# Two graph convolutions on one core: the order of a software-pipelined step, and a running maximum taken in another form

## The reference, cut to what matters

```
q = x @ qw + qb;  k = x @ kw + kb;  v = x @ vw + vb          # 8 heads of 16 channels
alpha = sum(q[dst] * k[src], channels) * SCALE               # one number an edge and head
m     = segment_max(alpha, dst)
a     = exp(alpha - m[dst]);  a = a / segment_sum(a, dst)[dst]
out   = segment_sum(v[src] * a, dst) + x @ sw + sb
...
h = relu(conv(x));  h = conv(h);  x = layernorm(x + h)
```

## Time and profile before

| | us |
|---|---|
| median of 3 runs | 3101.77 (3098.66 to 3106.87) |
| the profiled execution's own time | 3101.67 |
| its span, first to last instruction | 3099.9 |
| TensorE, busy | 2460.4 (79%) |
| VectorE, busy | 2586.2 (83%) |
| ScalarE, busy | 1926.8 (62%) |
| GpSimd, busy | 1987.3 (64%) |

### The profile page before, as it was taken

One profiled execution on the slowest core, in us unless ns is written; L12 is line 12 of the kernel. 1 busy time (PEld: TensorE's weight loads), 2 busy tenths in 40 slices (PEclk: granted clock), 3 DMA queues, 4 the chain that ended last, 5 costly groups with the idle time before them and its releaser, 6 DMA issues. The chain is left out here.

```text
span 3099.9 us, 46510 instructions
## 1 busy us (share of the span) xinstructions
PE 2460.4 (79%) x14327; PEld 1739.5 (56%) x14327; DVE 2586.2 (83%) x3231; ACT 1926.8 (62%) x3501; POOL 1987.3 (64%) x1891
## 2 busy tenths in 40 slices
PE   7899999959999996888888589999999961445620
PEld 3466666637777764565666356677777751223410
DVE  6689999969999996999999646898999885999940
ACT  0067677646666665988889557777777733455520
POOL 4477777714334326777777377788778416777776
PEclk9999999979999998999999899999999975657765
DMA  7456767656777765777777436799989777985311
GB/s 210 117 172 217 227 214 225 219 177 194 217 215 214 213 197 175 238 235 229 230 230 233 137 120 170 196 241 220 218 206 245 183 190 246 293 283 159 96 52 39
DMA packets 495871, 611.80 MB, mean 197 GB/s; under 512 B 67257, under 2 KB 285827, under 8 KB 495500
## 3 DMA queue, kind: packets, MB, share of 16 engines
q1 hardware_dynamic: 433814, 495.64, 53.2%
q0 software_dynamic: 56480, 111.88, 13.9%
q10 hardware_dynamic: 5334, 1.32, 0.2%
HBM read 391.94 MB, written 220.55 MB: 198 GB/s over the span
## 5 line engine op out<-in xcount | busy, mean ns | idle before, releaser
L781 POOL DMA_INDIRECT c_xs<-table_x,src_row x196 | 187.4, 956 | 264.5 <-PE c_psT L923 213.0
L1336 POOL DMA_INDIRECT g_xd_xs<-table_x,dst_row x196 | 226.4, 1155 | 122.6 <-issue 57.7
L771 POOL DMA_INDIRECT c_xs<-table_h,src_row x196 | 220.5, 1125 | 116.9 <-issue 78.8
L503 POOL DMA_INDIRECT xs<-in_x,src_i x196 | 227.0, 1158 | 86.2 <-issue 55.5
L488 POOL DMA_INDIRECT xd<-in_x,dst_i x196 | 217.3, 1109 | 94.8 <-issue 48.5
L1893 POOL DMA_INDIRECT out<-f_rows,end_i x196 | 197.4, 1007 | 67.3 <-issue 62.1
L1886 POOL DMA_INDIRECT f_rows<-table_x,src_row x196 | 190.8, 973 | 70.9 <-issue 59.4
L1336 POOL DMA_INDIRECT g_xd_xs<-table_x,src_row x196 | 196.3, 1001 | 59.8 <-issue 59.8
L1430 PEld LDWEIGHTS g_psP<-w_center,g_turns 128*128 128x128 f32 x1568 | 188.3, 194 | 69.4 <-ACT g_turns L1588 41.2
L1937 PE MATMUL f_psT<-w_ident,f_rows 128*128 128x128 f32 x196 | 47.6, 388 | 223.0 <-DVE f_rows L2030 223.0
L771 POOL DMA_INDIRECT c_xd<-table_h,dst_row x196 | 186.1, 949 | 59.7 <-issue 59.7
(11 more groups left out here) (345 smaller groups left out, 8350.2 us busy)
## 6 DMA issues: line engine op xcount, KB each, us to landing
g_share<-shares SPq DMA_DIRECT2D x196, 192.0 KB
xn<-in_x SPq DMA_DIRECT2D x49, 512.0 KB
table_x<-xo SPq DMA_DIRECT2D x49, 512.0 KB
table_x1b<-xb SPq DMA_DIRECT2D x49, 512.0 KB, 4.9
c_xn<-table_x SPq DMA_DIRECT2D x49, 512.0 KB
table_h<-c_xo SPq DMA_DIRECT2D x49, 512.0 KB
c_xn<-table_h SPq DMA_DIRECT2D x49, 512.0 KB
c_x1r<-table_x1b SPq DMA_DIRECT2D x49, 512.0 KB
```

The lines of the kernel that those rows point to most:

```text
L503: pool.indirect_dma_start(out=quarters(h.xs0[:, s, :])[j], out_offset=None, in_=io["x0"], in_offset=edge_index(h.src_i, n, j)).then_inc(h. ...
L771: pool.indirect_dma_start(out=quarters(rows[:, s, :])[j], out_offset=None, in_=table, in_offset=edge_index(columns, now.n, j)).then_inc(la ...
L781: pool.indirect_dma_start(out=quarters(xs[:, s, :])[j], out_offset=None, in_=table, in_offset=edge_index(h.src_row, now.n, j)).then_inc(sr ...
L1336: pool.indirect_dma_start(out=quarters(xd_xs[:, s, k, :])[j], out_offset=None, in_=table, in_offset=edge_index(columns, n, j)).then_inc(la ...
```

## The change

In both convolutions the maximum is taken in another form. The scan now gives, for each edge, the maximum over the edges before it, already lowered where a segment begins (`max` first, `add far` second); its first element comes from a small sum of its own (first_ready), and the value carried to the next tile is a small maximum (carry). One difference with the logits, drop, then gives both exponents by two clamps against zero: u = max(drop, 0), dropm = min(drop, 0).

In the second convolution alone:

- TensorE turns the edge rows of tile n+1 (`turn_edge_rows(soon)`) behind `alike` and ahead of `edge_products(last)`; before, they were turned at the head of the next step, behind the edge products. `own_rows` stands ahead of `values`.
- ScalarE scales a group one step later (`t.group(2)`), 4 blocks behind the copy of xdT and 8 at the end; p and c stand ahead of q and of the square.
- VectorE adds the edges' residual behind the clamps, and takes `norm_sum` between den and num.
- pre has 3 slots where it had 2, and the store of a group moves one step later on SyncE.

The wait for ee_ready ahead of xdT's copy is as it was.

```diff
@@ tensor
+            def turn_edge_rows(tile):
+                s = tile.slot
+                turn(0, tile, xs[:, s, :], src_landed[s], 64 * (tile.half + 1))
+                turn(1, tile, xd[:, s, :], dst_landed[s], 64 * (tile.half + 1))
...
             def alike(now):
                 pe.wait_ge(kq_ready, now.n + 1)
-                wait(pe, u_ready, now.n)
+                wait(pe, drop_ready, now.n)
+                wait(pe, carry_ready, now.n + 1)
...
-                    turn(0, now, xs[:, s, :], src_landed[s], 64 * (now.half + 1))
-                    turn(1, now, xd[:, s, :], dst_landed[s], 64 * (now.half + 1))
+                    if now.n == 0:
+                        turn_edge_rows(now)
...
-                    values(now)
                     own_rows(now, 0)
                     own_rows(now, 1)
+                    values(now)
                     alike(now)
+                if now and soon:
+                    turn_edge_rows(soon)
                 if last:
                     edge_products(last)
@@ scalar, second convolution
+                if old and a2 == 0:
+                    scale_rows(t, old, a2, b2, 0, 4)
+                if last:
+                    act.wait_ge(u_ready, last.n + 1)
...
+                    nc.scalar.activation(p[:, :], u[:, :], ACT.Exp, scale=-1.0).then_inc(p_ready, 1)
+                    act.wait_ge(dropm_ready, last.n + 1)
+                    wait(act, num_ready, last.n)
+                    nc.scalar.activation(c[:, :], dropm[:, :], ACT.Exp).then_inc(c_ready, 1)
+                if now:
+                    keep_q(now)
                 if g:
...
-                if g:
-                    norm_scale(nc, act, h, g, a, b, var, lnv, rstd, var_ready, lnv_ready, rstd_ready, out_ready)
-                    if a == 0:
-                        scale_rows(t, g, a, b, 0, 3)
...
+                if old:
+                    scale_rows(t, old, a2, b2, 4, 12).then_inc(out_ready, 1)
                 if g:
-                    scale_rows(t, g, a, b, 3, 12).then_inc(out_ready, 1)
-            run_steps(2, step_spread if spread else step)
+                    norm_scale(nc, act, h, g, a, b, var, lnv, rstd, var_ready, lnv_ready, rstd_ready, out_ready)
+            run_steps(2 if spread else 3, step_spread if spread else step)
@@ vector, both convolutions
-                    here = bass.ds(last.n * TILE, TILE)
+                    here = bass.ds(last.n * TILE + 1, TILE - 1)
...
-                    nc.vector.tensor_tensor_scan(m[:, s, 1:TILE + 1], h.far[:, here], psA[:, :], m[:, s, 0:1],
-                                                 ALU.add, ALU.max).then_inc(m_ready, 1)
+                    nc.vector.tensor_tensor(m[:, s, 0:1], carry[:, :], h.far[:, bass.ds(last.n * TILE, 1)],
+                                            ALU.add).then_inc(first_ready, 1)
+                    dve.wait_ge(first_ready, last.n + 1)
+                    nc.vector.tensor_tensor_scan(m[:, s, 1:TILE], psA[:, 0:TILE - 1], h.far[:, here], m[:, s, 0:1],
+                                                 ALU.max, ALU.add).then_inc(m_ready, 1)
...
-                    nc.vector.tensor_tensor(u[:, :], psA[:, :], m[:, s, 1:TILE + 1], ALU.subtract).then_inc(u_ready, 1)
+                        nc.vector.tensor_scalar(dropm[:, :], drop[:, :], 0.0, None, ALU.min).then_inc(dropm_ready, 1)
...
+                        nc.vector.tensor_scalar(u[:, :], drop[:, :], 0.0, None, ALU.max).then_inc(u_ready, 1)
...
```

More of the change, by code:

```diff
@@ L866, in step @@
             def step(t):
-                now, last, (g, a, b) = t.tile(0), t.tile(1), t.group(2)
+                now, last = t.tile(0), t.tile(1)
                 soon = t.tile(-1)
@@ L896, in step @@
                 if layer:
-                    store_group(sp, g, a, b, t, result, xo, out_ready, node_stored, edge_stored)
+                    store_group(sp, *t.group(3), t, result, xo, out_ready, node_stored, edge_stored)
                     return
@@ L991, in step @@
             def step(t):
-                now, last = t.tile(0), t.tile(1)
+                now, last, soon = t.tile(0), t.tile(1), t.tile(-1)
                 if now:
                     s = now.slot
-                    turn(0, now, xs[:, s, :], src_landed[s], 64 * (now.half + 1))
-                    turn(1, now, xd[:, s, :], dst_landed[s], 64 * (now.half + 1))
+                    if now.n == 0:
+                        turn_edge_rows(now)
                     pe.wait_ge(turned_sb, 4 * now.n + 2)
@@ L1032, in scale_rows @@
                     ins = nc.scalar.activation(quarters(xo[:, g.slot, j // 4, :])[j % 4],
-                                               quarters(pre[:, g.slot, j // 4, :])[j % 4], ACT.Copy,
+                                               quarters(pre[:, g.at(3), j // 4, :])[j % 4], ACT.Copy,
                                                scale=rstd[:, g.slot, j:j + 1])
@@ L1079, in step @@
             def step(t):
-                now, last, (g, a, b) = t.tile(0), t.tile(1), t.group(1)
+                now, last, (g, a, b), (old, a2, b2) = t.tile(0), t.tile(1), t.group(1), t.group(2)
                 if now:
@@ L1096, in step @@
                     wait(act, var_ready, g.n)
-                    nc.scalar.activation(sq[:, a:b, :], pre[:, g.slot, a:b, :], ACT.Square).then_inc(sq_ready, 1)
-                if now:
-                    keep_q(now)
-                if last:
-                    act.wait_ge(dropm_ready, last.n + 1)
-                    wait(act, num_ready, last.n)
-                    nc.scalar.activation(c[:, :], dropm[:, :], ACT.Exp).then_inc(c_ready, 1)
-                    act.wait_ge(u_ready, last.n + 1)
-                    wait(act, pv_ready, last.n)
-                    wait(act, den_ready, last.n)
-                    nc.scalar.activation(p[:, :], u[:, :], ACT.Exp).then_inc(p_ready, 1)
+                    nc.scalar.activation(sq[:, a:b, :], pre[:, g.at(3), a:b, :], ACT.Square).then_inc(sq_ready, 1)
                 if now:
@@ L1164, in add_x1 @@
                     dve.wait_ge(x1e_landed[old.slot], 16 * (old.half + 1))
-                nc.vector.tensor_tensor(pre[:, g.slot, k, :], psE[k][:, :], x1r[:, g.slot, k, :],
+                nc.vector.tensor_tensor(pre[:, g.at(3), k, :], psE[k][:, :], x1r[:, g.slot, k, :],
                                         ALU.add).then_inc(pren_ready if k < 2 else pree_ready, 1)
@@ L1185, in step, with fall, height @@
                     wait(dve, dropm_ready, last.n)
-                    nc.vector.tensor_tensor(drop[:, :], m[:, s, 0:TILE], m[:, s, 1:TILE + 1],
-                                            ALU.subtract).then_inc(drop_ready, 1)
-                    wait(dve, p_ready, last.n)
-                    nc.vector.tensor_tensor(u[:, :], psA[:, :], m[:, s, 1:TILE + 1], ALU.subtract).then_inc(u_ready, 1)
+                    wait(dve, u_ready, last.n)
+                    nc.vector.tensor_tensor(drop[:, :], m[:, s, :], psA[:, :], ALU.subtract).then_inc(drop_ready, 1)
+                    nc.vector.tensor_tensor(carry[:, :], m[:, s, TILE - 1:TILE], psA[:, TILE - 1:TILE],
+                                            ALU.max).then_inc(carry_ready, 1)
                     dve.wait_ge(drop_ready, last.n + 1)
-                    wait(dve, c_ready, last.n)
-                    nc.vector.scalar_tensor_tensor(out=dropm[:, :], in0=drop[:, :], scalar=0.0, in1=h.far[:, here],
-                                                   op0=ALU.min, op1=ALU.add).then_inc(dropm_ready, 1)
-                    wait(dve, drop_ready, last.n)
-                    nc.vector.tensor_copy(m[:, 1 - s, 0:1], m[:, s, TILE:TILE + 1]).then_inc(carry_ready, 1)
+                    def fall():
+                        wait(dve, c_ready, last.n)
+                        nc.vector.tensor_scalar(dropm[:, :], drop[:, :], 0.0, None, ALU.min).then_inc(dropm_ready, 1)
+                    def height():
+                        wait(dve, p_ready, last.n)
+                        nc.vector.tensor_scalar(u[:, :], drop[:, :], 0.0, None, ALU.max).then_inc(u_ready, 1)
+                    height()
+                    fall()
+                if layer and b == 3:
+                    add_x1(t, g, 2)
                 soon = t.tile(-1)
@@ L1200, in step @@
                     times_q(now)
-                if layer and g:
-                    norm_sum(nc, dve, g, a, b, sq, var, sq_ready, var_ready, rstd_ready)
                 if last:
@@ L1215, in step @@
                                                  ALU.mult, ALU.add).then_inc(den_ready, 1)
+                if layer and g:
+                    norm_sum(nc, dve, g, a, b, sq, var, sq_ready, var_ready, rstd_ready)
+                if last:
                     dve.wait_ge(pv_ready, last.n + 1)
@@ L1232, in step @@
                     if g0:
-                        wait(dve, out_ready, g0.n - 1)
+                        wait(dve, out_ready, g0.n - 2)
                     for k in range(a0, min(b0, 2)):
```

18 lines of the change are left out of this document (9 added, 9 removed).

## The result

The changed kernel takes **3149.15 us** (median of 4 runs, 3144.63 to 3152.32); the kernel before, run beside it, 3100.78 (4 runs, 3098.66 to 3106.87). The ratio is 1.0153, with a 95% interval of 1.0136 to 1.0169: slower by 1.5%. The forecast was 3146, with 3126 to 3168 as its range.

A forecast was written before the change was run, and what follows sets the result against it. It took a loop through three engines to bound the second convolution, VectorE nearly full. Loop growth of 41 us, tail 2 and new neighbours 2 on 3101.7 gave 3146.7, predicted as 3146, range 3126 to 3168.

The forecast's parts named there:

- The loop: Second convolution: the path through TensorE, ScalarE and VectorE grows from 11.35 to 12.21 us a step, 41 us over 48 steps.
- edge products to the one that waits for them: Second convolution: 1.99 us from the edge products' first start until an instruction waiting for them starts, there VectorE's addition.
- four scalings, p, c and q: ScalarE, second convolution: work now between xdT's copy and the square, adding 2.78 us to the path.
- the reduction's move: VectorE, second convolution: reduction behind den takes pv and den, 1.85 us, off the path between square and kq.
- the early turns: TensorE, second convolution: turns ahead of edge products bring xdT's copy from 3.88 to 3.81 us behind alike, winning 0.07.
- The clamps: VectorE: 0.39 us each, net 0.1 to 0.3 less work a step; covered in the second convolution, 0 (-10 to +5) in the first.
- the tail and the rest: Stage end: about 2 us for one step's later scaling, plus 2 us for new pairs of neighbours.
- rival 2: GpSimd gathers, second convolution: run into more often; three stretched a tile give 13.0 us a step, 3181 us; chance 5%.
- Rival 1: VectorE sets the second convolution's pace and the change shortens it: step 10.9 us, 22 us less, 3080; chance 7%.
- Rival 3: Second convolution slows by half as ScalarE gaps close, or first convolution takes whole clamp gain: 3116 or 3136; chance 9%.
- Rival 4: Nothing moves: the effects cancel within 0.3% (9 us), needing 0.7 us a step off the loop; chance 3%.
- The clock, named as a danger: Second convolution: a granted clock below full, since TensorE stands still longer each step, would show the forecast wrong; no size.

The follow-up runs named there:

- e1: Changed kernel with three slots for xdT instead of two in the second convolution: 3099.13 us, ratio to before 0.9992, median step 11.17 us.
- e3: Changed kernel with all twelve scalings of a group at the end of ScalarE's step: 3102.84 us, median step 11.43 us.
- e7: Changed kernel with VectorE's reduction (norm_sum) put back ahead of pv and den: 3262.71 us, median step 14.14 us.
- e2: Changed kernel with the turns of xs and xd back at the head of the step, behind the edge products: 3145.75 us, median step 12.28 us.
- e5: Changed kernel with a third xdT slot and, on ScalarE, the square ahead of q: 3071.05 us, ratio to before 0.9907, median step 10.67 us.
- e6: Changed kernel with third xdT slot and square ahead of q, but the old maximum in both convolutions: 3105.26 us, ratio to before 1.0011.
- e8: Changed kernel with the old maximum in both convolutions, so the new order alone: 3147.84 us, median step 12.31 us.
- e9: Kernel before with only the turns of tile n+1 moved ahead of the edge products: 3113.87 us against 3092.49, median step 11.76 us.
- e10: Kernel before with the early turns and a third xdT slot: 3131.36 us against 3092.49, median step 11.76 us, mean 12.06.

## Why the prediction was right

**The loop.** 12.21 was forecast, 12.30 measured, and it is the loop that was laid down, term by term: `alike` 0.97 (0.96), turns 0.87 (0.86), edge products to the one that waits for them 2.05 (1.99), copy 0.49 (0.48), four scalings, p, c and q 2.78 (2.78), square 1.50 (1.51), reduction 1.67 (1.67), num 1.19 (1.18), kq 0.78 (0.78). The only term off by more than 0.01 is the edge products': 1.99 was VectorE's start behind them, and ScalarE starts 0.06 later. In time: 0.94 x 48 = 45 instead of 41. The profiled executions differ by 43.0 us and the medians by 48.4; 45 was forecast.

**The parts of the loop**, each by its own run: that the copy holds the loop, e1 (-1.13 us without the wait); that the scalings stand on the path, e3 (-0.87, of 1.17); that the reduction's move is worth 1.85, e7 (1.84); that the early turns change nearly nothing, 0.07, e2 (0.02 the other way). That q stands on the path too was shown with the third slot alone (e5 against e1, -0.50). No run moved p and c; their 1.04 us rests on the rows.

**The clamps.** 0.43 and 0.42 us long, 0.35 and 0.33 from start to start; the estimate was 0.39. Covered, as said: u ends 1.24 us ahead of p's start (0.7 to 1.0 was forecast). Net 0.1 to 0.3 us less VectorE work a step was forecast (its terms give 0.0 to 0.28): 0.23 by e5 and e6. For the first convolution 0 was forecast, with -10 to +5. No change shows. Its last aggregate came 3.0 us sooner, but from the first aggregate to the last it takes 447 to 452 us in the five kernels with the old maximum (before, e6, e8, e9, e10) and 445 to 455 in the seven with the new one. Its undisturbed step did become 0.10 shorter, 8.93 in all seven and 9.03 in all five, which "the order of TensorE is untouched" does not foresee; the steps that wait longer outweigh it. Which loop carries the 0.10 was not looked into.

**The end.** About 2 was put for the tail and the rest; the last aggregate to the last output tile is 1.5 longer, to the next layer's first matmul 2.3 (20.1 against 17.8).

**GpSimd** (rival 2) met one scan a tile: the gather at 1419.25 starts 0.11 us behind num's scan and lasts 1.91, as in the earlier trace rows, and it waits 1.4 us for a turn in most steps besides. The rival became real only once the loop was shorter: in e1, where its 11.14 a tile meet a step of 11.17. The gather that runs beside the clamps, at 1412.84, takes 1.09; in e8 the old differences run at that place, and the gather takes 0.94. By the Trainium skill (GPSIMD Engine Reference, section Key points) a VectorE instruction in a 2-port mode contends with GpSimd too; the trace agrees, and here it is 0.15 us, hidden. The prediction counted two new instructions of this kind. By the same sentence, which names two SBUF inputs as well, the old drop and dropm (far and m lie in SBUF) had been two already, so their number did not grow; beside them the gather took 0.94 in e8 and 1.21 to 1.39 in e6.

**The other rivals.** Rival 1 said that a hidden stretch from ee_ready to the square would leave VectorE's own pace, 10.9. The stretch was not hidden; where it is (e5), the pace is 10.67. Rival 3 was wrong in both halves: no gap on ScalarE closed up, and of the 10 us in the first convolution none can be told from scatter. Rival 4 needed 0.7 us off the loop and got -0.09. The clock, named as a danger, stayed full in the changed kernel.

**What was right by less than it looks.** The prediction called the early turns a gain of 0.07 by looking at ScalarE's copy alone. e9 shows that they cost 0.41 in the old order, through the third addition, which it passed over. That this stayed hidden here was luck, and its cause was not tested. The addition's new place is one candidate. The longer way of p is another: had the addition stood ahead of drop, u would have ended at about 1410.65 + 1.99 + 0.60 + 0.60 + 0.12 + 0.43 = 1414.39, an estimate from the edge products' start in the step above and the distances told here, and p, behind the copy and four scalings, starts at 1414.36 anyway.

## What to carry to other kernels

A wait on a slot costs nothing as long as the order of instructions hides it; when work is put ahead of what it waits for, look up each such guard and count the slots again. Here the guard kept the copy where it had been, so the early turns brought nothing. One more slot of 256 KB gave back 1.13 us of a 12.30 us step, and with the square ahead of q turned a loss of 1.5% into a gain of 0.9%. What made the loss is the 2.78 us of ScalarE's work put between the late copy and the square, against the 1.85 us that VectorE's new order took off. On an engine that works in order, what stands between the waiting instruction and the one that others wait for enters the loop in full: sort it by who is waited for, not by when its inputs are ready. A faster instruction on an engine (the clamps, 0.23 us a step) is worth its time only once that engine sets the pace, so remove the loop first and then compare.

## What was not expected of the hardware

The clock of TensorE. In e6, e7 and e10 the granted clock falls to half (1.2 of 2.4 GHz) for 3.4 us again and again within the second convolution, 16 times in e6, and 12 each in e7 and e10; in before, in the changed kernel and in the other runs it does not fall there until the stage's end. The mean granted clock from 1210 to 1735:

```profile
1210.00:1735.00 525.00, 440.99 (x2577) 335.87 (x2576) 503.82 (x647) 478.21 (x1105) 370.51 (x358) 0.95 0.73 227
```

That is e6, with 0.95; the changed kernel has 1.00:

```profile
1210.00:1735.00 525.00, 419.86 (x2398) 285.90 (x2397) 459.44 (x644) 433.66 (x1023) 379.82 (x347) 1.00 0.71 214
```

The busy time of TensorE in this stretch does not tell them apart: 441 us in e6 and 432 in e10, which fall, but 420 in the changed kernel, 438 in e9 and 451 in e1, which do not. Nor does the longest standstill of a step: between 1300 and 1600 it is 1.9 us in e6 and e7 and 1.2 in e10, which fall, but 1.65 in e5, which does not. (The changed kernel has three of 0.73 to 0.78 a step.) No run varied one of them alone, and the condition stays open. What it costs is shown: 1.45 us a step that it hits in e6, 1.64 in e7, 1.2 to 1.3 in e10. A gain of this size can be lost in this way, as e6 lost its own (3105 us and not some 3085), so compare the granted clock of a stage before its steps.
